# A two-layer decoder: spreading a softmax's inverse sums by DMA, and moving eight context projections and two gate steps

## What is computed

```python
x = layernorm(x + L0_attn(x))           # A0: 16 heads of 16 (causal)
x = layernorm(x + L0_xattn(x, ctx))     # X0: 16 heads of 16, 1024 keys
x = layernorm(x + L0_ffn(x))            # F: 256 -> 1024 -> 1024 -> 256, weights +-1
x = layernorm(x + L1_attn(x))           # A1: 16 heads of 64, 4 groups of keys; adds x once more
x = layernorm(x + L1_xattn(x, ctx))     # X1: 8 heads of 64, 1024 keys
x = layernorm(x + L1_moe(x))            # M: gates, 8 experts and a shared one
```

## Time and profile before

| | us |
|---|---|
| median of 3 runs | 1213.0 (1210.13 to 1213.84) |
| profiled execution | 1211.98 |
| its span | 1210.2 |
| PE busy in the span | 1094.6 (90%) |
| DVE busy | 744.2 (61%) |
| ACT busy | 550.9 (46%) |
| GpSimd busy | 111.0 (9%) |

### The profile page before, as it was taken

The page is one execution under the profiler, slowest core; times in us unless marked ns, Lnnn a source line. Parts: engine busy times, 40 slices in busy tenths (PEclk is TensorE's granted clock), DMA queues, the critical chain, the costliest instruction groups (busy, mean ns, idle before and its releaser), DMA issues.

```text
span 1210.2 us, 19630 instructions
## 1 busy us (share of the span) xinstructions
PE 1094.6 (90%) x7306; PEld 692.0 (57%) x7306; DVE 744.2 (61%) x1092; ACT 550.9 (46%) x1044; POOL 111.0 (9%) x133
## 2 busy tenths in 40 slices
PE   5999997788788988789989999999999999989997
PEld 3443353432222322268766777877777887768664
DVE  3431265679989998553326566465666776866257
ACT  2434333145445555832125566356644554555320
POOL 2011023020200000010001000010002000120020
PEclk9999997679989999899999999999999999989999
DMA  5514311020000000000035333123522633120001
GB/s 156 162 70 149 122 36 40 1 96 14 14 14 14 7 9 1 1 19 1 1 70 144 70 71 71 36 53 89 114 62 70 150 94 83 44 61 2 1 1 35
DMA packets 56493, 67.89 MB, mean 56 GB/s; under 512 B 14665, under 2 KB 35922, under 8 KB 56402
## 3 DMA queue, kind: packets, MB, share of 16 engines
q1 hardware_dynamic: 55234, 65.06, 20.5%
q10 hardware_dynamic: 1168, 1.57, 0.4%
HBM read 30.96 MB, written 13.63 MB: 37 GB/s over the span
## 4 chain that ended last, share of the span: by engine, by line
PE 72%; DVE 14%; issue 5%; ACT 4%; SPq 2%; DMA 2%; POOL 1%; ACTq 0%; DVEq 0%; POOLq 0%
PE p_ring L1723 11%; PE p_unit L1723 11%; PE p_out L1870 9%; PE p_ring L1767 8%; PE p_ring L1847 8%; PE p_ring L1744 6%; PE p_out L1836 5%; DVE halves L1494 5%; PE p_ring L1813 5%; DVE prob_a L1508 2%; PE p_ring L1791 2%; DVE x L1693 2%; PE p_unit L1948 1%; ACT prob_b L1294 1%; PE p_unit L1902 1%
## 5 line engine op out<-in xcount | busy, mean ns | idle before, releaser
L1308 ACT ACTIVATE prob_a<-p_ring 128x1024 f32<-128x1024 f32 x128 | 130.5, 1023 | 113.6 <-PE p_ring L1813 113.2
L1473 DVE TENSOR_REDUCE nmax<-p_ring 128x2 f32<-128x1024 f32 (+1 forms) x128 | 156.0, 1220 | 30.1 <-PE p_ring L1767 30.1
L1294 ACT ACTIVATE prob_b<-p_ring,nmax 128x512 f32<-128x512 f32 (+1 forms) x192 | 158.7, 837 | 32.5 <-DVE nmax L1473 32.1
L1326 ACT ACTIVATE probT_b<-p_ring 128x512 f32<-128x512 f32 x144 | 84.6, 599 | 195.3 <-PE p_ring L1847 193.7
L1494 DVE TENSOR_REDUCE halves<-p_ring 128x2 f32<-128x1024 f32 x128 | 155.6, 1219 | 26.7 <-PE p_ring L1791 26.2
L1767 PE MATMUL p_ring<-stacks 128*128 128x512 f32 x512 | 152.4, 420 | 9.5 <-ACT prob_b L1294 5.4
L1527 DVE COPY probT_b<-p_ring 128x512 f32<-128x512 f32 x112 | 77.1, 688 | 118.3 <-PE p_ring L1847 117.9
L1847 PE MATMUL p_ring<-ident,prob_b 128*128 128x128 f32 x1024 | 136.0, 276 | 4.8 <-DVE probT_b L1527 4.4
L1847 PEld LDWEIGHTS p_ring<-ident,prob_b 128*128 128x128 f32 x1024 | 117.3, 142 | 28.5 <-issue 20.1
L1813 PE MATMUL p_ring<-x_q,x_kq 32*128 32x512 f32 x512 | 120.1, 660 | 1.9 <-DVE halves L1494 1.6
L1494 DVE TENSOR_REDUCE wide_max<-p_ring 128x2 f32<-128x256 f32 (+3 forms) x64 | 52.6, 823 | 95.5 <-PE p_ring L1785 95.3
(11 more groups left out here) (208 smaller groups left out, 1536.9 us busy)
## 6 DMA issues: line engine op xcount, KB each, us to landing
stacks<-splitH_b SPq DMA_DIRECT2D x80, 128.0 KB, 2.3
stacks<-splitL_b SPq DMA_DIRECT2D x80, 128.0 KB, 2.4
stacks<-x_kd SPq DMA_DIRECT2D x32, 256.0 KB, 4.7
x_kd<-early SPq DMA_DIRECT2D x8, 512.0 KB, 3.1
x_v<-x_vd SPq DMA_DIRECT2D x8, 512.0 KB, 3.9
x_vd<-early SPq DMA_DIRECT2D x6, 512.0 KB, 2.8
a_st<-a_image SPq DMA_DIRECT2D x32, 64.0 KB, 2.8
x_kd<-xT SPq DMA_DIRECT2D x4, 512.0 KB, 3.1
```

Of the source, the lines that this page charges most:

```text
L1294: ins = nc.scalar.activation(prob_b[:, n % NP_SLOTS, a * 512:a * 512 + w_all], p_scores[:, n % 2, a * 512:a * 512 + w_all], ACT.Exp, bias= ...
L1308: nc.scalar.activation(prob_place(key), slot_of("S2", key), ACT.Exp, accum_out=x0_sums[:, m:m + 1]).then_inc(done["E2"], 1)
L1473: nc.vector.tensor_reduce(nmax[:, n % 4, 0:heads], src, AX.X, ALU.max, negate=True).then_inc(done["M"], 1)
```

## The change

- **Inverse sums by DMA.** For all groups but the last, RC makes only the reciprocal. A new step RS on SP stores `rsum` to a small buffer in HBM (`b_sums`, two DMAs of 512 single elements, one for each half of the rows), waits until they have landed, and reads it back by two broadcasts to 64 partitions each, into one of two slots of `spread`. No transposes and no copy of ACT are left for these groups.
- **Outputs raw.** A new step OC (DVE) copies `p_out` to `outT_b` unscaled; the next group's AV waits for OC. ON is now a multiply in place on GpSimd, put two rounds after the group's last AV in the list. The last group keeps the transposes, with OC and then ON on DVE.
- **Doubles.** Of the 18 units in the chain of `x1_context` the first ten keep round 24 as their earliest; the last eight get 66, 69, ... 87.
- **Gates.** For batch 0, ZD 1 is not before `starts(21) + 9` and ZD 2 not before `starts(21) + 13`.

The diff, without its repeated context:

```diff
     heads = [list(c) for c in chains]
-    late = []
+    late, scaled = [], []
+    last_group = tiles[-1][:3]
...
     n, crowded = 0, False
-    while n < len(tiles) + LAG + 1 or any(heads) or pending or late:
+    while n < len(tiles) + LAG + 1 or any(heads) or pending or late or scaled:
         if n < len(tiles):
...
             sched.add(*late.pop(0))
+        while scaled and scaled[0][0] <= n:
+            sched.add(*scaled.pop(0)[1])
         empty()
...
             if i == TT - 1:
-                late.append(("ON", L, b, g))
+                late.append(("OC", L, b, g))
+                scaled.append((n + 2 if (L, b, g) != last_group else n, ("ON", L, b, g)))
         full = 0 <= m < len(tiles) and m % 2 == 1 and not crowded
...
             sched.add("RC", *group)
-            sched.add("UP", "rb", *group)
-            pending.append(("rb", *group))
-            placed = True
+            if group == last_group:
+                sched.add("UP", "rb", *group)
+                pending.append(("rb", *group))
+                placed = True
+            else:
+                sched.add("RS", *group)
         moved, held = True, []
...
         order = [u[1][1:] for u in x0_keys(1)] + order
-        return [unit(*u, at=24, after=[UA("v", "A0", 1, 1), UA("cT", 3, 1)]) for u in order]
+        return [unit(*u, at=24 if n < 10 else 66 + 3 * (n - 10), after=[UA("v", "A0", 1, 1), UA("cT", 3, 1)])
+                for n, u in enumerate(order)]
...
-        return [step("ZD", b, 0, after=[UD("mr", b)]), step("ZA", b, 0), step("ZD", b, 1), step("ZP", b),
-                step("ZD", b, 2, after=[("ZP", (b,))])]
+        apart = starts(21) if b == 0 else 0
+        return [step("ZD", b, 0, after=[UD("mr", b)]), step("ZA", b, 0), step("ZD", b, 1, at=apart and apart + 9), step("ZP", b),
+                step("ZD", b, 2, at=apart and apart + 13, after=[("ZP", (b,))])]
...
     bank_no = {u: i % 4 for i, u in enumerate(broad)}
-    groups = [key for kind, key in sched.steps if kind == "ON"]
+    groups = [key for kind, key in sched.steps if kind == "OC"]
+    last_group = groups[-1]
     early_places, early_uses = {}, [0] * EARLY
...
         early = [early0[:, :, :], early1[:, :, :], xT[:, :, T:2 * T]]
+        b_sums = nc.dram_tensor("b_sums", (2, 2, T), F32).ap()
         x1_kd = nc.dram_tensor("x1_kd", (B, 4, 128, NKV), F32).ap()
...
         x1_bo = put("x1_bo", [128, C])
-        spread = put("spread", [128, 512])
+        spread = put("spread", [128, 2, 512])
...
             "E2": "turned_probs_ready", "TM": "later_keys_cleared", "PV": "values_added", "KF": "operands_rounded",
-            "RC": "sums_inverted", "ON": "outputs_scaled", "UP": "unit_ready",
+            "RC": "sums_inverted", "ON": "outputs_scaled", "OC": "outputs_kept_raw", "UP": "unit_ready",
             "UA": "unit_emptied_by_act", "UD": "unit_emptied_by_dve", 
...
         a0_stacked = [sem(f"a0_stacked{s}") for s in range(HELD)]
+        sums_stored = [sem(f"sums_stored{s}") for s in range(2)]
+        sums_spread = [sem(f"sums_spread{s}") for s in range(2)]
         a0_spread = [sem(f"a0_spread{b}") for b in range(B)]
...
                           .then_inc(x0_held[place], 16)
+                if kind == "RS":
+                    G = group_no[key]
+                    slot, turn = G % 2, G // 2
+                    wait(sp, "RC", *key)
+                    if turn:
+                        sp.wait_ge(sums_spread[slot], 16 * 2 * turn)
+                    for a in range(2):
+                        sp.dma_start(b_sums[slot, a].rearrange("(i p) -> p i", p=128), rsum[:, slot, :, a],
+                                     allow_slow_non_contiguous=True).then_inc(sums_stored[slot], 16)
+                    sp.wait_ge(sums_stored[slot], 16 * 2 * (turn + 1))
+                    if turn:
+                        wait(sp, "ON", *groups[G - 2])
+                    for a in range(2):
+                        sp.dma_start(spread[64 * a:64 * a + 64, slot, :], b_sums[slot, a].partition_broadcast(64))\
+                          .then_inc(sums_spread[slot], 16)
                 if kind == "VL":
...
                     nc.gpsimd.tensor_copy(x0_kqF[:, n % HELD], x0_kq[:, n % HELD]).then_inc(done["KF"], 1)
+                elif kind == "ON" and key != last_group:
+                    g = key[2]
+                    G = group_no[key]
+                    wait(pool, "OC", *key)
+                    pool.wait_ge(sums_spread[G % 2], 16 * 2 * (G // 2 + 1))
+                    nc.gpsimd.tensor_tensor(outT_b[:, g, :], outT_b[:, g, :], spread[:, G % 2, :], ALU.mult)\
+                      .then_inc(done["ON"], 1)
                 elif kind == "XH":
...
                         G = group_no[u[1:]]
-                        if G:
-                            wait(act, "ON", *groups[G - 1])
-                        ins = nc.scalar.activation(spread[:, :], p_unit[:, :], ACT.Copy)
+                        wait(act, "ON", *groups[G - 2])
+                        ins = nc.scalar.activation(spread[:, G % 2, :], p_unit[:, :], ACT.Copy)
                     elif u[0] == "xT" and u[1] == "X0":
...
                     ng = LAYERS[key[0]]["G"]
-                    link(nc.vector.reciprocal(rsum[:, G % 2, :, 0:ng], sums[:, G % 2, :, 0:ng]))
-                    if G:
-                        wait(dve, "UP", "rb", *groups[G - 1])
-                    else:
-                        early_stored(dve, 1)
-                    nc.vector.tensor_copy(rwide[:, :, :].rearrange("p i (a r) -> p i a r", a=ng),
-                                          rsum[:, G % 2, :, 0:ng].unsqueeze(3).to_broadcast([128, TT, ng, 128 // ng]))\
-                      .then_inc(done["RC"], 1)
-                elif kind == "ON":
+                    if G >= 2:
+                        dve.wait_ge(sums_stored[G % 2], 16 * 2 * (G // 2))
+                    ins = nc.vector.reciprocal(rsum[:, G % 2, :, 0:ng], sums[:, G % 2, :, 0:ng])
+                    if key == last_group:
+                        link(ins)
+                        ins = nc.vector.tensor_copy(rwide[:, :, :].rearrange("p i (a r) -> p i a r", a=ng),
+                                                    rsum[:, G % 2, :, 0:ng].unsqueeze(3).to_broadcast([128, TT, ng, 128 // ng]))
+                    ins.then_inc(done["RC"], 1)
+                elif kind == "OC":
                     L, b, g = key
-                    G = group_no[key]
-                    wait(dve, "UA", "rb", *key)
                     wait(dve, "AV", *key, TT - 1, parts(key[0]) - 1)
...
                         wait(dve, "UP", "wo", *prev_batch[(L, b)], 1)
-                    nc.vector.tensor_tensor(outT_b[:, g, :], p_out[:, :], spread[:, :], ALU.mult)\
+                    nc.vector.tensor_copy(outT_b[:, g, :], p_out[:, :]).then_inc(done["OC"], 1)
+                elif kind == "ON" and key == last_group:
+                    g = key[2]
+                    G = group_no[key]
+                    wait(dve, "UA", "rb", *key)
+                    wait(dve, "OC", *key)
+                    wait(dve, "ON", *groups[G - 1])
+                    nc.vector.tensor_tensor(outT_b[:, g, :], outT_b[:, g, :], spread[:, G % 2, :], ALU.mult)\
                       .then_inc(done["ON"], 1)
...
                     if i == 0 and part == 0 and G:
-                        wait(pe, "ON", *groups[G - 1])
+                        wait(pe, "OC", *groups[G - 1])
                     if i == 0:
```

## The result

The changed kernel takes 1255.5 us (1252.2 to 1259.4, four runs) against 1212.2 before: ratio 1.0357, 95% interval 1.0334 to 1.0381. Slower by 43 us, where the forecast was 30 us faster and the range ended at 1197. The profiled execution has a span of 1255.9 us.

The account below looks back on a forecast made before the run. PE was taken to bound the second layer (busy 97.8 of 100 us). Gains 11.5 + 2.5 + 1.3 + 7.4 + 9.0 - 2.0 = 29.7 us gave a forecast of 1182.5 us, range 1169 to 1197.

Parts of the forecast that it names:

- L: SP's wait for the element stores to land in HBM: taken as 3.6 us, with 8.8 from a queued broadcast load.
- SP's sum: SP's time per second-layer group: 4.95 stack loads + 2.5 issues + 3.6 landing = 11.1 us, fitting in 13.2.
- The first rival: SP becomes the bound in A1's 15 groups, each losing the landing time beyond 5.7 us; 1228 at 8.8; chance 0.05.
- Collisions: Second layer: later key rounding, later stacks and collisions together charged 2.0 us (0 to 4).
- Slack of the stacks: Stack loads start about 2 us later but are used four rounds, 14 us, later, so slack is left.
- Transposes: 23 second-layer groups lose four transposes, 0.50 us of PE each: 11.5 us, plus 2.5 from waits on ACT's copy.
- the freed unit slot: Pair 11's query unit goes before batch 0's output projections, its stacks load earlier: 1.3 us of PE wait back.
- Doubles: Eight doubles leave rounds 38 to 48 for 68 to 91: 18 us saved, 9 paid, net 9 (-6 to +17).
- the second rival: Clock drops in thinned rounds 38 to 48 and new place stays half speed: no gain or 3 lost, 1191 to 1195; chance 0.16.
- Gates: At GpSimd's power near 1068 us, separating the steps returns 4.4 us of PE idle and 3.0 of clock: 7.4.
- GpSimd: GpSimd gets 23 two-input multiplies of 128x512, 1.2 us each, which can hold one key rounding by 1.2 us.
- 2.5 us of slack: At A1's first batch end the product is ready at 766.0, the projection at 768.5, so the chain is hidden.

Follow-up runs that it names:

- the best one above: The changed kernel with stored sums in 16-byte elements and SP's wait and broadcasts two rounds later, behind the stack loads: 1182.5 us, ratio 0.9770 to the kernel before.
- the base: The changed kernel without its inverse sums by DMA, so only the eight doubles moved and the gate steps apart: 1193.6 us, ratio 0.9846 to the kernel before.

## Why the prediction was wrong

**The failed step: L, the landing of the stores.** I took 3.6 us, from a load of 256 four-byte elements. It was about 9.2. SP's sum of 11.1 us in a group of 13.2 became 10.3 + 1.1 + 5.0 = 16.4. The first rival's formula comes near where it applies: at L = 9.2 it gives 15 x (9.2 - 5.7) = 52 us for A1, where the changed kernel loses 46.7 to the best one above (273.8 against 227.1), 38.4 of them by the wait. It has no term for X1, where 26.0 are lost (244.2 against 218.2) and 24.0 of them stay when the wait is moved. Together 72.7 us; the two profiled executions differ by 71.2 and the medians by 73.0. I had the upper bound 8.8 and gave the rival 0.05, because the two rows seemed to speak of a queue's depth and of a small transfer. Both were *reads*. No row that I had showed a write of single elements side by side into HBM. The anatomy section of the Trainium skill's page "DMA: Bandwidth & Descriptors" says that completion can take surprisingly long when the target is HBM. With dense elements the runs agree: 7.5 us into HBM and 2.0 into SBUF for the same 128 elements. But the same 128 placed 64 bytes apart in HBM land in 1.5 us, so HBM as the target is not enough. The Trainium skill's rule in the section "Rules for kernel authors" of that page, one descriptor per element for a strided last dimension, does not carry the price here: 512 spaced elements a store cost 4.6 us in all (1198.2 against 1193.6), and land in 2.2. An end of a range that rests on a row of another kind is an end, and deserved more than 1 in 20.

**The missing term: traffic.** "Collisions" were 2.0 us (0 to 4) for everything. Stores still landing delayed a stack load of another queue by 7.5 us and cost 30.6 us on the base with no wait at all. With the wait moved, they cost 31.8 (1214.3, against 1182.5 for the same kernel with 16-byte elements), and they are nearly all of X1's loss. The prediction saw the queue in front of SP and not the transfers in flight beside it.

**Slack of the stacks.** I had them "used four rounds, 14 us, later". That does not hold everywhere. At the start of A1's second batch PE waits for a stack 1.9 us after its last issue even in the base; there a delay goes straight to the end.

**Transposes: right.** 0.50 us of PE and what hangs on ACT's copy: groups of A1 go from 14.0 to 13.1 us (from 693.18 to 707.18 in the base, from 692.37 to 705.44 with 16-byte elements); predicted 13.2. With the 1.3 us of the freed unit slot I had 11.5 + 2.5 + 1.3 - 2.0 = 13.3, and the stage of the best kernel is 12.9 shorter than the base's. The make-up differs a little, so part of the agreement is luck: PE was busy 444.3 us in the stage and now 431.5, 12.8 less, while its waits sum to 13.8 us in both. Those for ACT's exponentials fell from 3.3 to 1.9 and the one for a stack (1.4) is gone, but those for DVE's statistics rose from 1.2 to 3.7 and 1.5 came for its copies. With the wait in its place (16-byte elements alone) 6.7 us show in the stage, 458.3 to 451.6: three groups, the last but one of A1 and two of X1, are 1.4 to 3.4 us longer than in the best kernel.

**Doubles: right.** Predicted 18 saved at the old place and 9 paid at the new one. The score of round 52 starts at 161.19 before and at 141.70 now, 19.5 us earlier; at A1's start 10.2 are left, so 9.2 were paid. Alone they gave 10.5. The clock was not full as I hoped: 0.85 from 116 to 150 us, where it had been 1.00 (in the direction of the second rival, without its price), and 0.93 from 200 to 250 us, where it had been 0.70 (0.66 and 0.74 in the earlier trace rows):

```profile
116.00:150.00 34.00, 32.26 (x219) 16.51 (x220) 20.80 (x27) 11.83 (x16) 5.80 (x12) 0.85 0.10 32
200.00:250.00 50.00, 43.75 (x212) 20.41 (x210) 36.13 (x50) 18.47 (x28) 9.20 (x11) 0.93 0.32 111
```

**Gates: right.** 7.4 predicted, 6.3 measured, with the interval from 5 to 11; both terms, idle and clock, are there.

**GpSimd: near.** 23 products took 1.38 us each, 1.2 predicted. At the batch ends, where I counted 2.5 us of slack, PE waited 5.4 us in two waits: the stores took 9 us to land and not 3.6.

## To carry to other kernels

Before a queue gets a step that waits for a DMA, find a row of that very kind, write to HBM or read, element size and layout; a row of another kind is only a bound, and the chance of the rival that hangs on it should say so. Make small stores in 16-byte pieces, or spaced, and turn the order back where the data is read by an engine. Price a DMA twice: once for the engine that waits for it, and once for the loads that are in flight beside it, in other queues too. The two can be told apart as here: one kernel with the DMA issued and nobody waiting, one with the wait.

## What I had not expected of the hardware

- 128 four-byte elements side by side in HBM land in 7.5 us; 64 bytes apart in 1.5; in one row of SBUF in 2.0. 128 of 16 bytes side by side take 1.9.
- While such stores of 512 elements land, other transfers come late: copies from SBUF to SBUF on another queue were used 9.4 us after their last issue, where it was 1.9; key loads from HBM issued just before the stores 12.1 us after, where it was 4.6; a load of 128 KB from HBM took some 12 us and not some 8.5.
- GpSimd reading the broadcast sums at a stride of 16 bytes made its product 1.75 us long on average, where it was 1.38, and did no harm: plain groups stayed at 13.1 us.
- Two DMAs issued by ScalarE cost 0.6 us in every plain group of A1, though ScalarE is busy 55 of 100 us there.
